# A conditioned transformer chain, batch by batch: q, k and v as three products of split operands, two masks moved to ScalarE, three buffers for the hyper weights

## What is computed

```python
# layer 0: adaptive RMS norm, attention (16 heads of 16), residual; then norm, SwiGLU, residual
h = gamma_a * rmsnorm(x) + beta_a
q, k, v = h @ W_q.T, h @ W_k.T, h @ W_v.T
attn = softmax(sqrt(16 / 256) * q k^T)                    # per head
x = x + alpha_a * (attn v) @ W_o.T
h = gamma_f * rmsnorm(x) + beta_f
x = x + alpha_f * (silu(h @ gate.T) * (h @ hidden.T) @ out.T + out_b)
# layer 1: norm, gated GELU, quantised hidden layer times ternary weights, residual
# layer 2: adapter whose weights are made per batch by a "hyper" product of the condition
# layer 3: layer norm with a bias from the condition
```

## Time and profile before

| | |
|---|---|
| median of 3 runs | 997.89 us (997.86 to 999.56) |
| profiled execution | 996.25 us, its span 994.4 us |
| PE busy | 959.8 us, 97% of the span |
| PE weight loads | 789.1 us, 79% |
| VectorE busy | 746.2 us, 75% |
| ScalarE busy | 565.4 us, 57% |
| GpSimd busy | 230.1 us, 23% |
| DMA | 89.43 MB, mean 90 GB/s |
| chain that ended last | PE 86%, DMA 4%, VectorE 4% |

### The profile page before, as it was taken

How to read it: one execution, slowest core, us unless ns; L and a number is a source line. 1 busy time by engine, 2 the same in 40 slices (tenths; PEclk the granted TensorE clock), 3 DMA queues, 4 the chain that set the end, 5 groups by cost and what they waited for, 6 DMA issues and landing times.

```text
span 994.4 us, 20904 instructions
## 1 busy us (share of the span) xinstructions
PE 959.8 (97%) x6602; PEld 789.1 (79%) x6602; DVE 746.2 (75%) x1731; ACT 565.4 (57%) x1164; POOL 230.1 (23%) x301
## 2 busy tenths in 40 slices
PE   8788999999999999999999999999999999998997
PEld 7356679797878879797888879797888879796876
DVE  5734568888878788787878787887878787885756
ACT  3265655647466665647466555747565565745532
POOL 2163403121212213121211213121221213111220
PEclk8778999999999999999999999999999999999999
DMA  7998660221304040221304040220304031120000
GB/s 223 287 320 313 240 213 8 84 68 45 106 1 149 1 138 11 86 63 44 106 1 149 1 131 19 75 73 34 115 1 149 1 119 31 65 75 1 23 17 17
DMA packets 75777, 89.43 MB, mean 90 GB/s; under 512 B 16529, under 2 KB 62113, under 8 KB 73185
## 3 DMA queue, kind: packets, MB, share of 16 engines
q1 hardware_dynamic: 70816, 71.19, 23.6%
q0 software_dynamic: 1440, 9.18, 2.5%
q10 hardware_dynamic: 3488, 8.65, 2.4%
HBM read 63.14 MB, written 25.31 MB: 89 GB/s over the span
## 4 chain that ended last, share of the span: by engine, by line
PE 86%; DMA 4%; DVE 4%; issue 2%; ACT 2%; SPq 1%; POOL 0%; ACTq 0%; DVEq 0%; POOLq 0%
PE bank L742 18%; PE bank L806 15%; PE bank L756 9%; PE bank L701 7%; PE bank L711 6%; PE bank L683 6%; PE bank L654 5%; PE bank L719 3%; PE bank L823 3%; PE bank L663 2%; DMA hyper<-w_hyper 2%; PE bank L633 2%; PE bank L843 2%; PE bank L816 1%; PE bank L728 1%
## 5 line engine op out<-in xcount | busy, mean ns | idle before, releaser
L568 POOL TENSOR_TENSOR act_lo<-act_f,act_hi 128x256 fp32r<-128x256 f32 x120 | 88.2, 735 | 368.1 <-ACT act_hi L1190 368.1
L1454 DVE TENSOR_REDUCE neg_max<-bank 128x2 f32<-128x512 f32 x256 | 161.9, 681 | 0.0
L1147 ACT ACTIVATE probs<-bank 128x512 f32<-128x512 f32 x256 | 135.3, 601 | 24.2 <-PE bank L701 11.8
L1226 ACT ACTIVATE gelu_g<-bank,r 128x256 f32<-128x256 f32 x128 | 60.7, 475 | 94.6 <-PE bank L806 93.3
L1184 ACT ACTIVATE silu_g<-bank 128x256 f32<-128x256 f32 x128 | 49.2, 385 | 104.9 <-PE bank L742 104.5
L742 PE MATMUL bank<-h_hi,gh_hi 128*128 128x256 f32 x512 | 104.1, 285 | 2.8 <-DVE h_lo L1517 2.8
L742 PE MATMUL bank<-h_lo,gh_hi 128*128 128x256 f32 x512 | 103.6, 284 | 0.0
L742 PE MATMUL bank<-h_hi,gh_lo 128*128 128x256 f32 x512 | 103.3, 283 | 0.0
L1523 DVE TENSOR_TENSOR act_f<-bank,silu_g 128x256 f32<-128x256 f32 x128 | 53.6, 419 | 61.5 <-ACT silu_g L1184 61.5
L1190 ACT ACTIVATE act_hi<-act_f 128x256 fp32r<-128x256 f32 x128 | 53.4, 417 | 75.8 <-DVE act_f L1523 74.0
L742 PEld LDWEIGHTS bank<-h_hi,gh_hi 128*128 128x128 f32 x512 | 83.6, 190 | 11.2 <-issue 6.2
(11 more groups left out here) (213 smaller groups left out, 2016.5 us busy)
## 6 DMA issues: line engine op xcount, KB each, us to landing
q_stack<-q_dram SPq DMA_DIRECT2D x96, 128.0 KB
k_stack<-k_dram SPq DMA_DIRECT2D x90, 128.0 KB
q_dram<-probs SPq DMA_DIRECT2D x16, 512.0 KB, 2.8
k_dram<-probs SPq DMA_DIRECT2D x16, 512.0 KB, 2.8
hyper<-w_hyper POOLq DMA_DIRECT2D x8, 1024.0 KB, 9.6
hyper<-w_hyper SPq DMA_DIRECT2D x8, 1024.0 KB, 7.3
x_res<-xT SPq DMA_DIRECT2D x16, 256.0 KB, 2.8
out<-xc SPq DMA_DIRECT2D x15, 256.0 KB, 2.5
```

Of the source, the lines that this page charges most:

```text
L568: pool.tensor_tensor(act_lo[:, c % 3, :], act_f[:, c % 2, :], act_hi[:, c % 3, :].bitcast(F32), ALU.subtract).then_inc(g_lo.sem, 1)
L1147: act.activation(probs[:, h % SLOTS], halves(SCORE_BANKS[h]), ACT.Exp, scale=float(H / D) ** 0.5).then_inc(s_exp.sem, 1)
L1226: act.activation(gelu_g[:, n % 2, :], halves(7 - n % 2)[:, 1, :], ACT.Gelu, scale=r3[:, t:t + 1])\
L1454: dve.tensor_reduce(neg_max[:, qt, :, pair:pair + 1].rearrange("p a o -> p (a o)"), halves(n % 3), AX_X, ALU.max, negate=True).then_inc(ma ...
```

## The change

q, k and v of batches 2 to 15 are made from split operands. ScalarE rounds `w_qkv` once to `w_qkv_hi`, in step 1, and VectorE puts the rest into `w_qkv_lo`, which lies where `w_qkv` lay. For each batch GpSimd rounds `h1` to `h1_hi` and makes `h1_lo` in the place of `h1` (`split_a`, ahead of `sum_x`). Each product becomes three of fp32r. Batches 0 and 1 stay as they are. To find the space, the fourth hyper buffer goes (load 5 then waits for product 2 and is issued behind `low_part(0)` and `low_part(1)`), and `sq3`, `h3_lo`, `h3_hi` and `mlp_y` lie in buffers of other stages. In the attention's second half (u = 1), ScalarE masks the first tile (`masked`, behind the exponentials) into `den_raw` and `o_norm`; `attend` 2 and 3 write to banks 3 and 4 instead of two halves of bank 3.

```diff
-        w_qkv = sb("w_qkv", [P, DC, 3 * D])
+        with ExitStack() as whole_qkv:
+            w_qkv = sb("w_qkv", [P, DC, 3 * D], stack=whole_qkv)
+        w_qkv_lo = sb("w_qkv_lo", [P, DC, 3 * D], F32R)
+        w_qkv_hi = sb("w_qkv_hi", [P, DC, 3 * D], F32R)
...
-            return n % 4 if n < 6 else n % 2
+            return n % 3 if n < EARLY else n % 2
...
-        sq3 = sb("sq3", [P, DC, T])
-        h3_lo = sb("h3_lo", [P, DC, T], F32R)
+        sq3 = silu_g
+        h3_lo = act_lo[:, 0:DC, :]
...
-        h3_hi = sb("h3_hi", [P, DC, T], F32R)
+        h3_hi = act_hi[:, 0:DC, :]
...
-        mlp_y = sb("mlp_y", [P, TT, D])
+        mlp_y = gelu_g
...
-            if n >= 4:
-                eng.wait_ge(hyper_mm.sem, n - 3 if n < EARLY else n - 1)
+            if n >= 3:
+                eng.wait_ge(hyper_mm.sem, n - 2 if n < EARLY + 2 else n - 1)
...
+                def split_a(b):
+
+                    pool.wait_ge(n1_dve.sem, n1_dve.at(b))
+                    pool.tensor_tensor(pool_idle, pool_idle, pool_idle, ALU.mult)
+                    pool.tensor_copy(h1_hi[:], h1[:]).then_inc(h1_split.sem, 1)
+                    pool.wait_ge(h1_split.sem, h1_split.at(b, 1, back=2))
+                    pool.tensor_tensor(h1_lo[:], h1[:], h1_hi[:].bitcast(F32), ALU.subtract).then_inc(h1_split.sem, 1)
...
+                    if f and nxt:
+                        split_a(nxt)
+                    if g:
                         sum_x(g)
...
-                for n in range(2, EARLY):
+                for n in range(2, EARLY - 1):
                     hyper_load(pool, n)
                 low_part(0)
                 low_part(1)
+                hyper_load(pool, EARLY - 1)
                 low_part(2)
...
+                    if in_parts(b):
+                        pe.wait_ge(h1_split.sem, h1_split.at(b, back=2))
+                        pe.wait_ge(qkv_lo.sem, 1)
+                        return [(w, h, c) for w, h in ((w_qkv_hi, h1_hi), (w_qkv_lo, h1_hi), (w_qkv_hi, h1_lo)) for c in range(DC)]
...
-                    at = halves(2 + t // 2)
+                    at = (halves(2)[:, 0, :], halves(2)[:, 1, :], halves(3)[:, 0, :], halves(4)[:, 0, :])[t]
...
+                def masked(b):
+
+                    tile = halves(3)[:, 0, :]
+                    act.wait_ge(pv_mm.sem, pv_mm.at(b, 3))
+                    act.wait_ge(o_dve.sem, o_dve.at(b, 3))
+                    act.activation(den_raw[:], tile, ACT.Copy, scale=rows_of[:, 1:2]).then_inc(o_act.sem, 1)
+                    if b.follows():
+                        act.wait_ge(wo_mm.sem, wo_mm.at(b, back=1))
+                    act.activation(o_norm[:, 1, :], tile, ACT.Copy, scale=rows_of[:, 0:1]).then_inc(o_act.sem, 1)
...
+                        if starts(f) and c == 3:
+                            act.activation(w_qkv_hi[:], w_qkv[:], ACT.Copy).then_inc(qkv_hi.sem, 1)
...
+                    if a:
+                        masked(a)
...
+                        if starts(f) and c == 5:
+                            dve.wait_ge(qkv_hi.sem, 1)
+                            dve.wait_ge(v_mm.sem, v_mm.at(Batch(1)))
+                            dve.tensor_tensor(w_qkv_lo[:], w_qkv[:], w_qkv_hi[:].bitcast(F32), ALU.subtract).then_inc(qkv_lo.sem, 1)
```

More of the change, by code:

```diff
@@ L136, in build @@
         par_a2 = sb("par_a2", [P, 3, DC])
-        h1 = sb("h1", [P, DC, T])
+        with ExitStack() as whole_h1:
+            h1 = sb("h1", [P, DC, T], stack=whole_h1)
+        h1_lo = sb("h1_lo", [P, DC, T], F32R)
+        h1_hi = sb("h1_hi", [P, DC, T], F32R)
         y1 = sb("y1", [P, T])
@@ L279, in build @@
         w_hi, w_hi_dve, w_lo = sem("w_hi"), sem("w_hi_dve"), sem("w_lo")
-        hyper_in = [sem(f"hyper_in{i}") for i in range(4)]
+        hyper_in = [sem(f"hyper_in{i}") for i in range(3)]
         hyper_late = [sem(f"hyper_late{i}") for i in range(2)]
@@ L648, in project_qk @@
                         pe.wait_ge(s_exp.sem, s_exp.at(b, back=1))
+                    terms = qkv_terms(b)
                     for x, done in ((0, q_mm), (1, k_mm)):
@@ L1463, in normalise @@
                     even, odd = rows_of[:, 0:1], rows_of[:, 1:2]
-                    tile, num = halves(2 + u), o_norm[:, u, :]
+                    first, second = ((halves(2)[:, 0, :], halves(2)[:, 1, :]), (halves(3)[:, 0, :], halves(4)[:, 0, :]))[u]
+                    num = o_norm[:, u, :]
                     dve.wait_ge(pv_mm.sem, pv_mm.at(b, 2 * u + 2))
@@ L1470, in normalise @@
                         dve.wait_ge(o_dve.sem, o_dve.at(b, back=1))
-                    dve.tensor_scalar(den_raw[:], tile[:, 0, :], odd, None, ALU.mult).then_inc(o_dve.sem, 1)
-                    dve.wait_ge(o_dve.sem, o_dve.at(b, k + 1))
-                    dve.scalar_tensor_tensor(den_raw[:], tile[:, 1, :], even, den_raw[:], ALU.mult, ALU.add).then_inc(o_dve.sem, 1)
+                    if u == 0:
+                        dve.tensor_scalar(den_raw[:], first, odd, None, ALU.mult).then_inc(o_dve.sem, 1)
+                        dve.wait_ge(o_dve.sem, o_dve.at(b, k + 1))
+                    else:
+                        dve.wait_ge(o_act.sem, o_act.at(b, 1))
+                    dve.scalar_tensor_tensor(den_raw[:], second, even, den_raw[:], ALU.mult, ALU.add)\
+                        .then_inc(o_dve.sem, 1 if u == 0 else 2)
                     dve.wait_ge(o_dve.sem, o_dve.at(b, k + 2))
@@ L1476, in normalise @@
                     dve.stream_shuffle(den[:], den_raw[:], [(DH + i) % 32 for i in range(32)]).then_inc(o_dve.sem, 1)
-                    dve.tensor_scalar(num, tile[:, 0, :], even, None, ALU.mult).then_inc(o_dve.sem, 1)
-                    dve.wait_ge(o_dve.sem, o_dve.at(b, k + 4))
-                    dve.scalar_tensor_tensor(num, tile[:, 1, :], odd, num, ALU.mult, ALU.add).then_inc(o_dve.sem, 1)
+                    if u == 0:
+                        dve.tensor_scalar(num, first, even, None, ALU.mult).then_inc(o_dve.sem, 1)
+                        dve.wait_ge(o_dve.sem, o_dve.at(b, k + 4))
+                    else:
+                        dve.wait_ge(o_act.sem, o_act.at(b, 2))
+                    dve.scalar_tensor_tensor(num, second, odd, num, ALU.mult, ALU.add)\
+                        .then_inc(o_dve.sem, 1 if u == 0 else 2)
                     if between:
```

31 lines of the change are left out of this document (17 added, 14 removed).

## The result

The changed kernel took 993.60 us (median of 11 runs, 989.41 to 995.88), the kernel before 998.84 beside it (11 runs, 996.25 to 1002.38): ratio 0.9937, 95% interval 0.9921 to 0.9953. It is faster, by about half of the 11.1 us of the forecast, and outside its range. Run again later, the same two kernels gave 990.74 and 999.61: 0.9919 (0.9896 to 0.9941). Two single executions were far slower (2341.46 us in "masks only", 1295.1 in "waits first"); they count in those two medians and not in the ratios.

What follows compares the result with a forecast made beforehand. PE, 97% busy, bounds the kernel, with VectorE's normalising chain nearly tied before L719. 9.75 (13 batches) + 0.52 + 0.52 + 0.31 = 11.1 off 996.25 gives 985.15, plus 1.64 to the median: 986.8 us, range 983.0 to 989.8.

Steps and rivals of the forecast that it cites:

- Two chains within 0.13 us, saved together: Ahead of L719, PE's own work and VectorE's normalising arrive within 0.13 us; what one saves alone is worth nothing.
- Fp32r products at 0.118: In q, k and v, four products of 0.432 become twelve of 0.118: 1.42 for 1.73, PE saving 0.31 each.
- 0.19 of a switch: In q's first product, 0.19 us taken as a switch from the 32-column matmuls ahead of it; it stays.
- v and what follows L719: After L719, v saves PE 0.31 per batch, less 0.08 charged for a late act_u and waits between engines.
- GpSimd's split, ScalarE's queue: h1's split costs nothing, 5.8 us to spare; ScalarE's two masked copies, 0.94 us, leave 0.25 before the logarithm.
- rivals 3 and 4: 3: ScalarE's longer queue delays L719, about 1002 us, chance 0.03. 4: late GpSimd split or added PE waits, 997, chance 0.04.
- 2 as far as ScalarE goes: Rival: ScalarE late by a little, or the start loses 1 to 3 us through load 5; 990 us, chance 0.13.
- A steady batch gains 0.75: Each of 13 steady batches gains 0.52 + 0.31 - 0.08 = 0.75 us, 9.75 in all.
- the add starts where the mask did: VectorE's normalising chain loses its first mask, so o_norm is ready and L719 begins 0.52 us earlier.
- The cold clock of step 15 gone: Shorter idle time before step 15's L719 no longer drops PE's clock: 1.4 to 1.6 us less, not in the sum.
- rival 1: PE alone decides, 0.93 per batch (2.3 us more), and a cold clock goes: together 981.5 us, chance 0.17.
- "0.52" for step 0: Step 0 has no q, k, v product; PE's wait of 2.94 us for o_norm shortens by 0.52.

Runs made afterwards that it cites:

- masks only: Kernel before with only the two masks on ScalarE and the changed banks, q, k, v undivided, four hyper buffers: 996.81 us, 0.9971 of before.
- waits first: Changed kernel with VectorE's waits on ScalarE's two masked products put ahead of its wait on the last attention product: 992.73 us, 0.9925 of before.
- par_f early: Step 1's par_f load issued ahead of the residual's load: on the changed kernel 986.07 us (0.9877), again 989.14 (0.9902); on the kernel before 995.52 (0.9956).
- the fourth load behind: Changed kernel with par_f early, plus step 0's fourth weight load issued on ScalarE behind v's copy and the high parts: 988.37 us, 0.9890 of before.
- split only: Changed kernel with the masks back on VectorE and the banks put back, so split q, k, v and three hyper buffers: 1000.40 us, 0.9993 of before.

## Why the prediction was right or wrong

*Two chains within 0.13 us, saved together.* Right, and shown by the parts alone: from q to the projection 0.10 and 0.00, together 0.41.

*Fp32r products at 0.118.* Right: v's twelve take 1.42, and q's and k's start at the same pace, two in 0.23 to 0.24. (The "0.19 of a switch" in q was the view's bookkeeping: by the starts of the records q and k took 1.83 each. It entered no saving.) *v and what follows L719.* Right: 0.31 - 0.08 = 0.23 forecast, 0.20 to 0.22 measured in the rest of the period. *GpSimd's split, ScalarE's queue.* Right, both with more room than needed; rivals 3 and 4 fell, and 2 as far as ScalarE goes. Its other half, a start that loses 1 to 3 us, is in size what came, but load 5 alone doesn't show it (1.0002, at most 1.5 us).

*A steady batch gains 0.75.* Too much: 0.63. The step that failed is the 0.52 of the normalising chain, "the add starts where the mask did". The mask had started 0.06 us after the last attention product's end (518.38, 518.44); the add starts 0.19 after it, behind the register operation and the wait on ScalarE's mask. The prediction had left that wait out. The stretch shortened by 0.41, and by 0.50 once the waits on ScalarE stood ahead. From step 1 to step 15 there are 14 such intervals: forecast 9.75 + 0.31 + 0.52 = 10.6, measured 8.6 to 8.9 (55.97 + 731.07 and 56.03 + 730.77 against 55.16 + 723.00).

*The end, and around the span.* The cold clock of step 15 gone, priced at 1.4 in rival 1 and left out of the sum, did come in some executions: to the end, 76.75 and 77.22 against 78.18 and 79.10. On the mean of all profiles of either kind (11 with both parts, 5 without the split) it is 77.6 against 78.6, so 1.0. Outside the span every kernel with the split took 2.2 to 2.3 us, before 1.8 to 1.9, masks only up to 2.0: 0.4 lost, for which no term stood and whose cause is open. The time around the span was taken over from before's execution.

*The start.* This step failed most: "0.52" for step 0 and "0, between -1 and +2" for everything done once. 8.8 + 1.0 - 0.4 = 9.4 us are gained behind step 1's L748, and the ratios show 6.3 and 8.1 (0.9937 and 0.9919 of 1000); the first one's interval, 4.7 to 7.9, leaves 9.4 out. The difference, 1.3 to 3.1, was given back ahead of it, where 0.5 was to be gained. Step 0's chain is shorter as forecast (PE waited 2.46 for o_norm instead of 2.94), but step 1's L748 came at 133.5 on the mean of four profiles with both parts against 130.5 of four without the split, par_f late in all. On the mean of the profiles (eleven with both parts, five without the split) two pieces grew: from step 0's L748 to product 6, 17.0 us against 16.0, and from product 11 to step 1's L748, 22.6 against 21.6. They are the pieces with the two coins in them. Whether the change loads the coins or had bad throws isn't shown. Not the cause: the once-only work on w_qkv (hidden whole) and par_f (both kernels lose by it); three buffers and the late load 5 can be a part of it, up to 1.5 us. What is, within this scatter, stays open; most of the first profile's 8.2 us are accidents of one execution: par_f's 3.87 and the slow last load, some 2.

*The baseline.* I summed against the time of a profiled execution and kept its 1.64 us to the median of three runs; its opening was one of the lucky ones, though its clock too fell behind the gate product. Eleven runs put before's median 1 us higher. That made no difference to the sign, but the second profile of before would have shown that its opening moves by more than the terms I argued about there.

## What to carry to other kernels

Where two chains end within a tenth of a microsecond, cut both or neither, and price the join anew: work moved to another engine comes back as a wait, and its place among the waits counts (0.09 of 0.50 us here). Take such differences from the starts of records: where one chain runs through and the other has waited, the pieces of the chain of waits are cut in different places. An opening in which weights are loaded beside the first steps needs its own ledger: take a second profile of the unchanged kernel before arguing about 2 us there, and when an edit of the changed kernel gains, run it on the unchanged one too before calling it the missing part. A cost that doubling shows is the cost of the second helping; whether the first is paid is read from the spacing of what it could delay. All that gained together (par_f early, the fourth load behind, waits first) ran at 987.46 us, 0.9876 of before, faster than both kernels.

## What the runs showed of the hardware

- par_f, a transfer of 3 KB, took 8.9 to 12.3 us to land in the nine profiles in which it was issued at 77 to 81 us, beside and behind 1 MB loads (12.12 in after's first), and 3.0 to 5.6 in the nine in which it was issued at 70 to 73, ahead of them (5.29 in par_f early).
- A wait whose value is worked out on registers, standing behind the wait that arrives last, cost the chain 0.09 us (waits first: 0.19 to 0.10).
- An undivided fp32 projection, eight records, took 1.73 us from its first start to the next instruction's where PE ran into it from its own work (masks only), and 1.83 where it didn't (before, split only, after).
- The same idle time went with either clock. At step 15's projection 2.0 to 2.1 us of it went with full clock in six profiles and with a fall in six; 2.77 us ahead of the gate products of step 0 with 1.00 in one (before with par_f early) and with 0.50 in others (before's first).
